# Sixteen leading blocks, plain block writes with accumulating gathers, and the shared expert's first products moved into TensorE's waits, in a recurrence-plus-MoE layer on one Trainium2 core

## Chip, cores and metric

The program runs on one NeuronCore of one Trainium2 chip. The metric is device time in microseconds. The kernel before takes 448.93 us, the median of three runs (447.82, 448.93, 449.15).

## What is computed

Input x is 4 sequences of 512 tokens with 256 features, all fp32. The layer is

```python
x = x + attn(layernorm(x))        # a gated complex linear recurrence over the 512 tokens
x = x + ffn(layernorm(x))         # a mixture of 32 experts and a shared expert
# ffn, for xf of 2048 tokens x 256:
scores = sigmoid(xf @ gate_w.T)                     # 32 experts in 8 groups
# the 4 groups with the highest maximum, in them the 6 best experts, weights normalised to 2.5
y = sum over the 6 chosen e of  w[e] * (silu(xf @ w11[e].T) * (xf @ w33[e].T)) @ w22[e].T
shared = (silu(xf @ sw1.T) * (xf @ sw3.T)) @ sw2.T  # inner width 256
out = y + shared
```

## The kernel before

Each engine has its own program, written out by hand: `block.sync` (SP, which only issues transfers), `gpsimd` (POOL), `scalar` (ACT), `vector` (DVE) and `tensor` (PE). Semaphores tie them together, so the order of the stages in each list is the order of the work.

**The front part** goes over the tokens in six chunks (`CHUNKS`, L45) of 256, 256, 512, 512, 256 and 256 tokens. For each chunk it makes the first layer norm, the projection, the gates, the recurrence (two scans on DVE), the output product (`residual_in`, L1106, and `out_project`, L1115), the second layer norm, the router's logits (`logits`, L1091) and scores, the choice of six experts (`choose`, L817) and, by products with a triangle of ones on PE (`positions`, L1125), the place of each token in its expert's list in DRAM (`places`, L859). Then POOL scatters the token's row to its six places (`scatter_rows`, L421): one indirect transfer for each tile of 128 tokens and choice, 96 in all, each of 128 rows of 320 floats (256 features, 32 weights and 32 row numbers).

**The table.** When all places are known, DVE works out which 128-row blocks of which expert are to be run in which order (L926 to L953), 127 blocks at most. The order runs by phases (`PHASE_ENDS`, L47), so that blocks holding early tokens come first. Three small products turn the table into a row (L1191 to L1193), which is copied to `tabs` (L955).

**The shared expert** is done by sequence b and half h: `shared_gate_up(b, h)` (L1160, four products of 512 columns), ACT's silu (L607), DVE's `shared_hidden` (L957), `shared_down(b)` (L1169, eight products of 256 columns) and DVE's `shared_out` (L962). In PE's program the pairs (0,0) and (0,1) stand behind the last `logits`, then `positions(4)` and `positions(5)`, the table, and all the rest.

**The loop over 127 blocks** is pipelined in steps. SP loads a block's rows (`load_block`, L352, up to eight ahead), PE transposes them (`rows_t`, L1216), multiplies by gate and up weights (`gate_up`, L1223) and by the down weights (`down`, L1232). ACT copies weights and takes silu. DVE multiplies (`hidden`, L982) and scales the output (`block_out`, L987). POOL scatters the 128 output rows to `choice_rows` in DRAM (`scatter`, L436), six rows a token side by side, one indirect transfer a block. When a phase is through, SP loads a tile's six rows a token (`load_choices`, L361, 768 KB), and DVE adds them to `resid` with six additions of 128x256 (`add_choice`, L1010), interleaved with the steps by `LOAD_AT` and `ADD_AT`. Tile 14 is summed on PE (L1261). Finished tiles are stored by ACT and SP.

Before its first block, SP waits for the table and for all 96 row scatters:

```python
            sp.wait_ge(s_tab, 1)
            sp.wait_ge(s_pad, 16)
            sp.wait_ge(s_outp, NCH)
            for i in range(NCH):
                sp.wait_ge(s_scat[i], 16 * TOPK * CHUNKS[i][2])
```

and PE waits for the four additions of the shared expert (`s_resid`) before the first transpose.

## Time and profile before

| | |
|---|---|
| three runs, median | 448.93 us |
| profiled execution: its own time | 450.83 us |
| profiled execution: span, first to last instruction | 449.1 us |
| PE busy / granted clock, mean | 376.1 us (84%) / 0.89 |
| DVE, ACT, POOL busy | 294.3, 260.7, 231.6 us |
| 127 scatters of block outputs on POOL | 127.0 us |
| 96 scatters of rows on POOL | 101.9 us |
| gate and up products of the blocks on PE | 134.9 us |

Times are from the span's start. A granted clock of 1.00 is 2.4 GHz, 0.50 is 1.2 GHz. In a timeline row the first number is the start, the second the length (of a merged run of instructions, start to end). In square brackets stands how long the engine had been idle before it and who released it.

### The profile page before, as it was taken

What the parts mean: (1) busy time and instruction counts of PE and PEld (TensorE: products, weight loads), DVE (VectorE), ACT (ScalarE), POOL (GpSimd) and SP (SyncE); (2) the same over time, 40 slices, a digit from 0 to 9 for tenths busy, and PEclk for the clock granted to TensorE, in tenths of its full rate; (3) what the DMA queues carried; (4) which work ended last, traced back from release to release, by engine and by line L of the source; (5) the groups of instructions that cost most, each with busy time, mean ns of one, the idle gap of its engine ahead of it and who ended that gap; (6) DMA issues with size and microseconds to landing.
All of it is one profiled execution on the core that took longest, in us unless ns stands there. A gap on an engine that the chain in (4) does not pass through costs nothing.

```text
span 449.1 us, 9145 instructions
## 1 busy us (share of the span) xinstructions
PE 376.1 (84%) x2120; PEld 301.2 (67%) x2121; DVE 294.3 (66%) x990; ACT 260.7 (58%) x585; POOL 231.6 (52%) x242
## 2 busy tenths in 40 slices
PE   2777696965976778399889999999999998998935
PEld 2644263745645563155579999999999997997924
DVE  3669688999988824612235555555567777777982
ACT  2678978768575132011157777767777776776710
POOL 2000000752778777777516666666656665663750
PEclk9898867595785687689999999999999999999996
DMA  8990000220335999333347666666689889879724
GB/s 241 405 339 2 0 0 1 74 102 15 118 118 201 413 430 380 130 128 128 117 145 215 188 195 182 204 188 191 191 265 354 255 248 300 303 208 336 244 83 174
DMA packets 41850, 87.70 MB, mean 195 GB/s; under 512 B 7204, under 2 KB 32295, under 8 KB 41296
## 3 DMA queue, kind: packets, MB, share of 16 engines
q1 hardware_dynamic: 28384, 54.77, 36.7%
q0 software_dynamic: 10704, 30.07, 18.6%
q10 hardware_dynamic: 2720, 2.40, 1.7%
q8 instruction: 15, 0.25, 0.3%
q14 instruction: 27, 0.22, 0.2%
HBM read 49.81 MB, written 39.71 MB: 199 GB/s over the span
## 4 chain that ended last, share of the span: by engine, by line
PE 50%; DVE 19%; ACT 9%; DMA 8%; issue 8%; POOL 3%; DVEq 1%; SPq 1%; ACTq 0%; POOLq 0%
PE PS L1228 17%; PE PS L1235 8%; PE PS L1165 7%; DMA payload_and_xn_t<-choice_rows 5%; PE PS L1220 4%; PE PS L1121 3%; POOL choice_rows L441 3%; PE PS L1178 3%; DMA resid<-in_x 2%; PE PS L1076 2%; ACT L605 1%; DVE st L682 1%; PE PS L1261 1%; ACT payload_and_xn_t L555 1%; DMA choice_rows<-block_out_s,block_meta 1%
## 5 line engine op out<-in xcount | busy, mean ns | idle before, releaser
L441 POOL DMA_INDIRECT choice_rows<-block_out_s,block_meta x127 | 127.0, 1000 | 86.0 <-issue 58.3
L427 POOL DMA_INDIRECT bucket_rows<-payload_and_xn_t,dest x96 | 101.9, 1062 | 116.2 <-DVE dest L874 88.2
L1228 PE MATMUL PS<-block_rows_t,block_gate_up_weights 128*128 128x128 f32 x1016 | 134.9, 276 | 0.0
L1228 PEld LDWEIGHTS PS<-block_rows_t,block_gate_up_weights 128*128 128x128 f32 x1016 | 123.4, 192 | 1.1 <-ACT block_rows_t L630 0.9
L625 ACT ACTIVATE block_gate_up_weights<-expert_weights 128x512 f32 x127 | 80.0, 630 | 35.6 <-issue 29.6
L1235 PE MATMUL PS<-expert_weights,block_hidden_t 128*128 x254 | 76.3, 382 | 3.8 <-DVE block_hidden_t L985 3.8
L992 DVE TENSOR_SCALAR block_out_s<-PS,block_meta 128x256 f32<-128x256 f32 x127 | 61.2, 482 | 0.0
L985 DVE TENSOR_TENSOR block_hidden_t<-block_silu_t,PS 128x128 f32<-128x128 f32 x127 | 36.3, 286 | 24.2 <-ACT block_silu_t L617 22.0
L630 ACT ACTIVATE block_rows_t<-PS 128x256 f32<-128x256 f32 x127 | 46.5, 366 | 7.6 <-PE PS L1220 7.6
L1220 PE MATMUL PS<-ident,block_rows_s 128*128 128x128 f32 x254 | 48.6, 273 | 1.4 <-DVE resid L964 1.3
L980 DVE COPY block_meta<-block_rows_s 128x2 f32 x127 | 22.0, 173 | 41.7 <-issue 41.4
L617 ACT ACTIVATE block_silu_t<-PS 128x128 f32<-128x128 f32 x127 | 35.0, 276 | 18.7 <-PE PS L1228 18.0
L1220 PEld LDWEIGHTS PS<-ident,block_rows_s 128*128 128x128 f32 x254 | 35.6, 141 | 14.5 <-DVE resid L964 1.7
L1016 DVE TENSOR_TENSOR resid<-resid,payload_and_xn_t 128x256 f32<-128x256 f32 x90 | 37.8, 421 | 10.1 <-DMA payload_and_xn_t<-choice_rows 9.2
L1235 PEld LDWEIGHTS PS<-expert_weights,block_hidden_t 128*128 128x128 f32 x254 | 38.5, 192 | 4.9 <-issue 4.9
L1165 PE MATMUL PS<-payload_and_xn_t,sw_s 128*128 128x512 f32 x64 | 33.3, 676 | 1.2 <-DVE turn_abs L960 1.2
L1121 PE MATMUL PS<-w_in_and_w_out,block_rows_s 128*128 128x256 f32 x96 | 25.8, 418 | 0.4 <-DVE block_rows_s L797 0.4
L1165 PEld LDWEIGHTS PS<-payload_and_xn_t,sw_s 128*128 128x128 f32 x64 | 13.8, 219 | 17.8 <-issue 16.0
L1076 PE MATMUL PS<-expert_weights,gate_blockdiag 128*128 128x256 f32 (+1 forms) x48 | 22.6, 634 | 1.7 <-ACT expert_weights L499 1.5
L1121 PEld LDWEIGHTS PS<-w_in_and_w_out,block_rows_s 128*128 128x128 f32 x96 | 20.3, 213 | 4.6 <-issue 0.7
L605 ACT ACT_TABLE_LOAD x18 | 23.1, 1283 | 0.3
L1087 PE MATMUL PS<-ident,payload_and_xn_t 128*128 128x128 f32 x32 | 7.4, 392 | 15.9 <-ACT payload_and_xn_t L555 12.0
(185 smaller groups left out, 459.1 us busy)
## 6 DMA issues: line engine op xcount, KB each, us to landing
block_rows_s<-bucket_rows SPq DMA_DIRECT2D x127, 160.0 KB
payload_and_xn_t<-choice_rows SPq DMA_DIRECT2D x16, 768.0 KB, 6.5
bucket_rows<-pad_rows SPq DMA_DIRECT2D x1, 5120.0 KB, 26.3
expert_weights<-in_experts SPq DMA_DIRECT2D x1, 4224.0 KB, 14.0
expert_weights<-in_experts SPq DMA_DIRECT2D x1, 3456.0 KB, 16.3
expert_weights<-in_experts SPq DMA_DIRECT2D x1, 2688.0 KB, 18.3
resid<-in_x SPq DMA_DIRECT2D x4, 512.0 KB, 9.3
choice_rows<-block_out_s,block_meta POOLq DMA_INDIRECT x127, 3.2
```

Source lines behind the costliest of these rows:

```text
L427: nc.gpsimd.indirect_dma_start(out=bucket_ap[:, :], out_offset=bass.IndirectOffsetOnAxis(ap=dest[:, t, k:k + 1], axis=0), in_=PAY[:, t, :] ...
L441: nc.gpsimd.indirect_dma_start(out=choice_ap[0:rows, :], out_offset=bass.IndirectOffsetOnAxis(ap=meta_id[:, slot, 1:2], axis=0), in_=yy[:, ...
L625: A(ws[:, r, :], W[:, bass.ds(first, KD * 2 * P)], ACT.Copy)
L630: A(xT[:, r, :], PS[:, r, 0:D], ACT.Copy).then_inc(s_xt, 1)
L985: TT(hh[:, r, :], sg[:, r, :], PS[:, 2 + r, P:2 * P], M).then_inc(s_hh, 1)
L992: TSC(yy[:, slot, :], PS[:, 6 + r, 0:D], meta[:, weight, 0:1], None, M).then_inc(s_y, 1)
L1016: ins = TT(resid[:, n, :], resid[:, n, :], RINGS[:, n % RING, k, :], AD)
L1121: ins = mm(PS[:, 6 + t // 2, (t % 2) * D:(t % 2 + 1) * D], PROD[h][:, t * P:(t + 1) * P], wt, start=False, stop=(n == len(parts) - 1 and t ...
L1165: ins = mm(PS[:, bank, :], sw13_s[:, k, g, h * P:(h + 1) * P], XN2T[:, b, k, :], start=(k == 0), stop=(k == KD - 1))
L1220: ins = nc.tensor.transpose(PS[:, r, k * P:(k + 1) * P], xs[:, slot, k * P:(k + 1) * P], ident[:])
L1228: ins = mm(PS[:, 2 + r, g * P:(g + 1) * P], ws[:, r, (2 * k + g) * P:(2 * k + g + 1) * P], xT[:, r, k * P:(k + 1) * P], start=(k == 0), st ...
L1235: mm(PS[:, 6 + r, 0:D], hh[:, r, :], W[:, bass.ds(w + KD * 2 * P, D)], start=True, stop=True).then_inc(s_yp, 1)
```

## The change

1. **Row format.** A row is 288 floats, with no row numbers. `choose` loses the scan and the addition that made them. It is cut in two stages, `choose_groups` and `choose_experts`.
2. **Block outputs.** SP writes each block's output with a plain transfer to 128 consecutive rows of `bucket_outputs`, at a row from a fourth row of the table (`write_block`, 11 blocks behind its load). SP reads its table entries four at a time. POOL's 127 scatters go. The tensor is cleared first, by five transfers from a zero tile.
3. **Token sums.** POOL gathers a tile's output rows, one indirect transfer for each choice, 96 of 128x256 in all. Choices 0 and 3 are added by the transfer into `resid`, 4 and 5 into the copies that 1 and 2 have made. DVE then makes two additions a tile in place of six. PE's sum and ACT's stores go, and SP stores. The places of the rows are worked out on DVE (`output_rows`, `output_sources`). Tile n is gathered once its phase is written and tile n - 4 is added.
4. **Leading blocks.** The first 16 blocks are full blocks of the first 8 tiles, found by `early_blocks`. SP loads them once the rows of chunks 0 to 2 have landed, and waits for the others before block 16. There are nine phases in place of five.
5. **Shared expert.** On PE the gate product of (0,0) goes before `residual_in(5)`, its up product between `ln2_transpose(4)` and `logits(4)`, and the two passes of (0,1)'s gate product into the gaps around `ln2_transpose(5)`. DVE makes the hidden rows of (0,0) and (0,1) between the stages of the last router chunks. The table's product stands behind the fifth pair.
6. **Loops** run over 8 steps in place of 16, and further.

```diff
-    PHASE_ENDS = (1, 2, 3, 4, 5)
+    CUTS = [[2], [2], [2, 4], [2, 4], [2], [1, 2]]
+    PHASE_TILES = [b * TS + t0 + cut for (b, t0, nt), cuts in zip(CHUNKS, CUTS) for cut in cuts]
...
+    RING = 4
+    SUMS = 3
+    EARLY_BLOCKS = 16
+    EARLY_TILES = 8
+    FIRST_ADD = 67
+    WRITE_LAG = NXS + 3
...
         def blocks_through(phase):
+            return max((PHASE_TILES[phase] * P * TOPK + E * (P - 1)) // P, EARLY_BLOCKS + E)
...
+            for n in range(NCH - 1):
+                part = slice(n * BLOCKS // (NCH - 1), (n + 1) * BLOCKS // (NCH - 1))
+                sp.wait_ge(s_gp, n + 1)
+                sp.dma_start(outputs_ap[part.start * P:part.stop * P].rearrange("(j p) d -> p j d", p=P),
+                             PADT[:, 0:D].unsqueeze(1).to_broadcast([P, part.stop - part.start, D])).then_inc(s_clear, 16)
...
+            rows_scattered(0, early_chunks)
...
+            def write_block(j, u):
+                if u % 4 == 0:
+                    sp.reg_load(first_outputs, tabs[0:1, bass.ds(j + 3 * P, 4)])
+                sp.wait_ge(s_y, j + 1)
+                row = sp.snap(first_outputs[u % 4], min_val=0, max_val=2 * P * P - P)
+                sp.dma_start(outputs_ap[bass.ds(row, P), :], yy[:, u % NY, :]).then_inc(s_ys[u % NY], 16)
...
+            for j in range(EARLY_BLOCKS):
+                load_block(j, j, j - NXS + 1 if j >= NXS else None)
+                if j >= WRITE_LAG:
+                    write_block(j - WRITE_LAG, j - WRITE_LAG)
+            rows_scattered(early_chunks, NCH)
...
+            def gather_outputs(n):
+                all_written(pool, blocks_through(phase_of(n)))
+                pool.wait_ge(s_src, n // TS + 1)
...
+                if n >= RING:
+                    pool.wait_ge(s_added, added(n - RING))
+                for k in range(TOPK):
+                    part = k % SUMS
+                    landed = s_cin[n % RING][part]
+                    into = resid[:, n, :] if part == 0 else RINGS[:, n % RING, part - 1, :]
+                    if k >= SUMS:
+                        pool.wait_ge(landed, 16 * (TOPK // SUMS) * (n // RING) + 16)
+                    nc.gpsimd.indirect_dma_start(
+                        out=into, out_offset=None, in_=outputs_ap[0:BLOCKS * P, :],
+                        in_offset=bass.IndirectOffsetOnAxis(ap=source[:, n, k:k + 1], axis=0),
+                        compute_op=ALU.add if part == 0 or k >= SUMS else ALU.bypass).then_inc(landed, 16)
...
-                dve.wait_ge(s_memb, i + 1)
-                flat_memb = memb[:, CHUNKS[i][1]:CHUNKS[i][1] + nt, :].rearrange("p t e -> p (t e)")
-                c.add(V.tensor_tensor_scan(rank[:, n, :].rearrange("p t e -> p (t e)"), flat_memb, flat_memb, 0.0, AD, ALU.bypass))
-                c.wait()
-                c.add(STT(PAY_id[:, rows, D + 1::2], rank[:, n, :], float((NT - 1 - tile) * P * TOPK),
...
-                    (ln2_stats, 5), (ln2_shift, 5), (choose, 4), (choose, 5), (places, 4), (places, 5)):
+                    (ln2_stats, 5), (ln2_shift, 5), (choose, 4), (choose_groups, 5),
+                    (first_product, 0), (choose_experts, 5), (places, 4), (first_product, 1), (places, 5),
+                    (early_blocks, 0)):
...
-            c.add(TT(PICKS, quant[:], PER_V.unsqueeze(1).to_broadcast([P, 3, V5]), M))
+            shared_out(0)
+            shared_hidden(1, 1)
+            c.add(TT(PICKS, quant[:], PER_V.unsqueeze(1).to_broadcast([P, 4, V5]), M))
...
+            def add_at(u, turn=None):
+                tile, k = u // (2 * TOPK) * 2 + u % (2 * TOPK) // ADDS, u % ADDS
+                if u % (2 * TOPK) < 2 * ADDS:
+                    add_sum(tile, k, turn)
...
-                    (out_project, 4), (positions, 3), (residual_in, 5), (out_project, 5), (ln2_transpose, 4),
-                    (logits, 4), (ln2_transpose, 5), (logits, 5)):
+                    (out_project, 4), (positions, 3), (first_gate, 0), (residual_in, 5), (out_project, 5),
+                    (ln2_transpose, 4), (first_up, 0), (logits, 4), (second_gate, 0), (ln2_transpose, 5),
+                    (second_gate, 1), (logits, 5)):
...
+            shared_part(0, 1, 1)
             positions(4)
+            shared_gate_up(1, 0)
             positions(5)
...
             for b in range(B):
-                if b + 1 < B:
+                if 0 < b and b + 1 < B:
                     shared_gate_up(b + 1, 0)
                 shared_down(b)
                 if b + 1 < B:
                     shared_gate_up(b + 1, 1)
+                if b == 1:
+                    block_table()
```

PE's program before, from the last `positions` ahead of the gap (L1135) to the products of the shared expert (L1165). `sw_s` are the shared expert's weights, `payload_and_xn_t` the normalised tokens:

```order
L1135 MATMUL PS<-member,ones 128x32 x4
L1111 MATMUL PS<-bout_s,ones_row 128x512
L1113 MATMUL PS<-resid,ident 128x256 x2
L1121 MATMUL PS<-w_in_and_w_out,block_rows_s 128x256 x4
L1121 MATMUL PS<-w_out_n,block_rows_s 128x256 x2
L1121 MATMUL PS<-w_in_and_w_out,block_rows_s 128x256 x2
L1087 MATMUL PS<-ident,payload_and_xn_t 128x128 x4
L1099 MATMUL PS<-gwt_s,payload_and_xn_t 128x32 x4
L1087 MATMUL PS<-ident,payload_and_xn_t 128x128 x4
L1099 MATMUL PS<-gwt_s,payload_and_xn_t 128x32 x4
L1165 MATMUL PS<-payload_and_xn_t,sw_s 128x512 x8
```

and the same place in the changed program (its lines L1289 are the shared expert's products):

```order
L1289 MATMUL PS<-payload_and_xn_t,sw_s 128x512 x2
L1257 MATMUL PS<-bout_s,ones_row 128x512
L1259 MATMUL PS<-resid,ident 128x256 x2
L1267 MATMUL PS<-w_in_and_w_out,block_rows_s 128x256 x4
L1267 MATMUL PS<-w_out_n,block_rows_s 128x256 x2
L1267 MATMUL PS<-w_in_and_w_out,block_rows_s 128x256 x2
L1233 MATMUL PS<-ident,payload_and_xn_t 128x128 x4
L1289 MATMUL PS<-payload_and_xn_t,sw_s 128x512 x2
L1245 MATMUL PS<-gwt_s,payload_and_xn_t 128x32 x4
L1289 MATMUL PS<-payload_and_xn_t,sw_s 128x512
L1233 MATMUL PS<-ident,payload_and_xn_t 128x128 x4
L1289 MATMUL PS<-payload_and_xn_t,sw_s 128x512
```

Six of the eight products that stood behind the last logits now stand in four places before them, two, two, one and one.

SP's program before, at the first two blocks. Each block reads the table once (L358) and issues one transfer:

```order
L358 TENSOR_LOAD tabs
L358 ISA x2
L359 ISA
L359 DMA block_rows_s<-bucket_rows 128x320
L358 TENSOR_LOAD tabs
```

and in the changed program, from the part of the loop that also stores tiles (`bucket_outputs` is what `write_block` writes, `out` the result):

```order
L382 TENSOR_LOAD tabs
L386 ISA
L387 DMA block_rows_s<-bucket_rows 128x288
L394 ISA
L395 DMA bucket_outputs<-block_out_s 128x256
L404 DMA out<-resid 128x256
L386 ISA
L387 DMA block_rows_s<-bucket_rows 128x288
L394 ISA
L395 DMA bucket_outputs<-block_out_s 128x256
```

SP now issues two transfers a block, or three where a tile is stored, and reads the table twice for four blocks, once for the loads and once for the writes.

## Rows read from the trace of the kernel before

**Rows 1.** Stretches of the loop on PE: length, PE busy, granted clock, DMA share, GB/s.
```profile
240.00:280.00 40.00, 40.00 (x313) 1.00 0.65 197
360.00:400.00 40.00, 38.49 (x293) 1.00 0.85 269
```

**Rows 2.** Timeline of PE, steps of the loop: start, length, line, operation, tiles.
```profile
230.31 0.38 PE L1220 MATMUL PS<-ident,block_rows_s 128*128 128x128 f32 x2
231.86 0.38 PE L1220 MATMUL PS<-ident,block_rows_s 128*128 128x128 f32 x2
...
426.83 0.38 PE L1220 MATMUL PS<-ident,block_rows_s 128*128 128x128 f32 x2
```

**Rows 3.** Waits in the loop: who waited for whom, us in total, times, longest.
```profile
PE PS L1235 <- DVE block_hidden_t L985: 3.8, 4, 1.5
```

**Rows 4.** Timeline of PE between the last positions and the loop.
```profile
153.03 2.04 PE L1111 MATMUL PS<-bout_s,ones_row 1*128 1x512 f32 x2 [2.03 <-ACT resid L546]
...
156.88 3.08 PE L1121 MATMUL PS<-w_in_and_w_out,block_rows_s 128*128 128x256 f32 x8
...
163.87 1.08 PE L1099 MATMUL PS<-gwt_s,payload_and_xn_t 128*128 128x32 f32 x8 [1.75 <-ACT payload_and_xn_t L562]
...
168.55 9.28 PE L1165 MATMUL PS<-payload_and_xn_t,sw_s 128*128 128x512 f32 x16
...
185.45 0.58 PE L1191 MATMUL PS<-ident,tabf 128*1 128x128 f32 x2 [6.02 <-DVE tabf L953]
...
188.12 6.31 PE L1165 MATMUL PS<-payload_and_xn_t,sw_s 128*128 128x512 f32 x8 [1.23 <-DVE turn_abs L960]
...
208.04 7.03 PE L1165 MATMUL PS<-payload_and_xn_t,sw_s 128*128 128x512 f32 x16
...
228.40 0.95 PE L1220 MATMUL PS<-ident,block_rows_s 128*128 128x128 f32 x4 [1.31 <-DVE resid L964]
```

**Rows 5.** Timeline of the end: PE's last down product, last output on DVE, last store.
```profile
430.74 0.69 PE L1235 MATMUL PS<-expert_weights,block_hidden_t 128*128 x2 [0.79 <-DVE block_hidden_t L985]
431.70 0.48 DVE L992 TENSOR_SCALAR block_out_s<-PS,block_meta 128x256 f32<-128x256 f32 x1
446.93 0.34 ACTq L668 DMA_DIRECT2D out<-block_rows_s  x1
```

**Rows 6.** Timeline of SP's queue, the first two loads.
```profile
224.26 1.48 SPq L359 DMA_DIRECT2D block_rows_s<-bucket_rows  x2
```

**Rows 7.** The indirect transfers on POOL: duration ns min/median/max, first and last start; then block outputs' landing.
```profile
L427 POOL DMA_INDIRECT bucket_rows<-payload_and_xn_t,dest x96: 956/960/2452, 79.4 to 220.7; - x96
L441 POOL DMA_INDIRECT choice_rows<-block_out_s,block_meta x127: 983/983/1242, 233.5 to 433.8; - x127
DMA to landing us min/median/max: 2.3/3.2/7.0
```

**Rows 8.** Two stretches on PE before and after its idle time at 151.
```profile
150.00:152.00 2.00, 0.77 (x16) 1.00 0.79 332
154.00:156.00 2.00, 2.00 (x4) 0.50 0.99 417
```

**Rows 9.** Timeline of DVE: row numbers, second norm, last places, the table's widest product.
```profile
150.55 0.41 DVE L855 TENSOR_TENSOR_SCAN rank<-member 128x128 f32<-128x128 bf16 x1
...
151.21 0.76 DVE L682 BATCH_NORM_STATS2 st<-PS 128x6 f32<-128x256 f32 x2
...
161.72 0.76 DVE L682 BATCH_NORM_STATS2 st<-PS 128x6 f32<-128x256 f32 x2 [5.55 <-PE PS L1121]
...
180.31 0.17 DVE L874 TENSOR_SCALAR dest<-dest_sorted 128x12 int32<-128x12 f32 x1
...
183.58 0.66 DVE L946 TENSOR_TENSOR block_rows_s<-block_quantities,block_rows_s 128x480 f32<-128x480 f32 x1
```

**Rows 10.** Timeline of ACT behind the last scores.
```profile
170.08 1.28 ACT L632 ACT_TABLE_LOAD   x1
```

**Rows 11.** The page, busy share of the DMA engines in tenths, 40 slices of 11.2 us.
```profile
DMA  8990000220335999333347666666689889879724
```

522 lines of the change are left out of this document (308 added, 214 removed).

## The prediction

> **What bounds the kernel now.** I read the stretches first, then the waits, then PE's timeline. The program has three parts. In the loop PE is the bound: it is busy all 40 us of a stretch [rows 1], and a step takes 231.86 - 230.31 = 1.55 us [rows 2] (1.546 by rows that repeat). From the third block's transpose to the last one's are 124 steps in 426.83 - 230.31 = 196.5 us [rows 2], where 124 x 1.546 would be 191.7, so the loop gives away 4.8 us, 3.8 of it where DVE, held up by its additions of loaded choices, brings `hidden` late [rows 3]. The first transpose starts at S = 228.4 and the last down product ends at T = 430.74 + 0.69 = 431.4 [rows 4, 5], so T - S = 203.0. The tail from T to the end at 449.1 is 17.7 us. Before S a chain of PE, ACT and DVE sets the time, and two things end together there: PE's first transpose waits for DVE's last shared addition [rows 4], and SP's loads start at 224.26 [rows 6], when the last of POOL's 96 scatters (start 220.7, 0.96 long [rows 7]) has landed. So neither the shared expert nor the scatters can be shortened alone. The change takes both.
>
> **Last out product.** PE idles 2.03 us at 151.0 and its granted clock falls from 1.00 to 0.50 [rows 4, 8]. `residual_in(5)` and half of `out_project(5)` then run at 1.2 GHz: bias and residual take 156.88 - 153.03 = 3.85 us, where the same instructions take 1.7 at full clock (two of 512 columns at 7.03 / 16 = 0.43, four of 256 at half of that, 0.22 [rows 4]). `first_gate` is four instructions of 512 columns, 1.7 us, and fits into the gap, so I expect the clock to stay at 2.4 GHz. The row numbers that `choose` loses cost DVE 151.21 - 150.55 = 0.66 us for a chunk of four tiles [rows 9], so what PE waits for comes 0.65 earlier. Then the residual ends at 152.75 + 1.7 = 154.5, DVE's products are there, and the out product takes 16 x 0.22 = 3.5: it ends at 158.0 in place of 161.7 [rows 9]. Gain 3.7.
>
> **Router of the last chunk.** `first_up` (1.7 us) fits into the wait of 1.75 before `logits(4)` [rows 4]. The two single passes (0.86 each) lie at ACT's norm and copy and may push `logits(5)` by 0.5. In DVE's order `first_product(0)` now stands ahead of `choose_experts(5)`. It waits for ACT's table load (1.28 [rows 10]) and silu, some 1.2 us, and everything of chunk 5 queues behind it. But before, `positions(4)` stood behind 9.28 us of products [rows 4], and now behind 1.7. By this schedule the last place is known at 174.1 in place of 180.5 [rows 9], so 2.7 more than the 3.7.
>
> **From the last place to the loop.** Before: 228.4 - 180.5 = 47.9 us, with PE idle 6.02 for the table and 1.23 behind it, and a pair at half clock, 6.31 in place of 7.03 / 2 = 3.5 [rows 4]. Now DVE has `early_blocks` (22 operations, mostly of 128 columns: the old table, 21 operations of 160 columns, took from 180.5 to 185.4 [rows 4, 9], so I take 4.7 us), then a table of 288 columns (6.3), then a product and a reduction of 1,152 columns (by 0.66 for 480 [rows 9], 1.35 each), and small ones. PE meanwhile does `shared_down(0)`, (1,1) and (2,0), and waits some 4.7 us for the hidden rows of (1,1), which stand in the middle of DVE's table work. After that PE has (2,1), the table, (3,0), down 2, (3,1), down 3 at 3.5 each, and DVE's `output_rows` (five operations of 512 columns, 4.1 us with the small ones) fits beside them. I get S = 212.0. The wait of 4.7 is long enough for the clock to fall, as the one of 6.02 did, and I add one pair at half clock, 3. The row numbers of chunks 0 to 2 come off a DVE that is over 90% busy there, 1.8 us in all, and I take 1.5 off. **S = 213.5, a gain of 14.9.** Loads must not stop this: SP's wait is now for chunk 2's scatters, which end near 161. The others may end at 224 as before: block 16 is wanted at 213.5 + 1.9 + 15 x 1.55 = 238.6, over 10 us later. Clearing 16.6 MB and the smaller rows cost nothing as long as the DMA engines are idle, as they are in the four slices from 34 to 79 us [rows 11]. Lost, that cover would only delay POOL, which has those 10 us.
>
> **The loop.** DVE has 32 additions in place of 90 and more, each placed 15 and more steps after its phase, so the 4.8 us go down to some 0.8: **T - S = 199.0, a gain of 4.0.** SP issues two transfers a step. A load came every 1.14 us (1.48 less one issue of 0.34 [rows 6]), of which 0.8 was the reading of the table. With two readings for four blocks that makes (8 x 0.34 + 2 x 0.8) / 4 = 1.1 us, with waits 1.2, under 1.55. If reading four entries saved nothing it would be 2 x 1.14 = 2.3, and the loop SP's, which the listed instructions speak against.
>
> **Gathers.** No row shows an accumulating gather. The nearest is the scatter of an output block: 0.98 on POOL plus the 0.30 that always lie between two, landing in 3.2, at most 7.0 [rows 7]. Below, a gather may cost the 0.96 of a row scatter. Above, the added reading of the destination may double the landing to 6.4. I take the scatter's values: choice 3 waits for choice 0's landing (3.2), which three issues (3 x 1.28 = 3.8) cover, so a tile takes t = 7.7. The pairs of tiles come every 12 steps (18.6 us), so POOL (15.4) keeps up. The engines' share was 0.65 without and 0.85 with the 768 KB loads [rows 1]. The same 12.6 MB now come in 1 KB rows, over more steps. The Trainium skill ("DMA: Bandwidth & Descriptors", Bandwidth) says to batch transfers to 1 MiB for over 75% of peak, which speaks against replacing 768 KB loads by 128 KB gathers. By that rule the gathers would land late under a filled set of engines, and the sum would be that of rival (a). The rows of before neither confirm nor deny it.
>
> **The tail.** Block 114 is written 13.6 us before T (its output at T + 0.75 - 12 x 1.55, and SP issues the write only after the load of block 125, plus landing). From there POOL gathers tiles 12 and 13 until T + 2, then tile 14 (which waits for tile 10's additions, the last of the loop) until T + 9.7, and tile 15's last gather starts at T + 16.1. Landing 3.2, one addition 0.4, store 449.1 - 446.93 = 2.2 [rows 5]: **T + 22.0, a loss of 4.3** against 17.7.
>
> **Sum.** 449.1 - 14.9 - 4.0 + 4.3 = 434.5 for the span. The median of the runs, 448.93, is 0.2 below this span (the profiled execution's own time, 450.83, is 1.9 above the median), so the time is **434.3 us**.
>
> **Rivals.**
> (a) *Gathers set the end, slower.* If an accumulating gather lands in L over 3.9 us, choices 3, 4 and 5 each wait for it and a tile takes L + 3.9. POOL starts at S + 81.8 (block 47 written), and the end is S + 81.8 + 16 (L + 3.9) - 1.3 + L + 2.75 = S + 145.7 + 17 L. It decides from L = 4.4, is slower than before from L = 5.4, and at L = 6 gives 461. For it: landings up to 7.0 under load [rows 7], two reads for each write. Against it: the median of 3.2 at nearly the same rate. The same page (SWDGE vs HWDGE vs iDMA) says that DVE in its two-port mode locks GpSimd out of the memory in which it writes descriptors. Here POOL's instruction rose to 2.45 once in the front part, but not above 1.24 in the loop [rows 7], and DVE does less there now. Chance 0.17, with a loop held by SP or the DMA engines (each 0.1 us a step is 13 us) in it.
> (b) *The front part gives little.* If `first_gate` runs long or late, the clock falls all the same, and DVE's longer table work (some 14 us more than before with the output rows) sets S: the 3.7 and half of the 10 go, S = 222, end 443. Chance 0.15.
> (c) *No effect.* The leading blocks do nothing unless the table comes before the scatters' end, and the gain of the front would be eaten by a tail of 30 us: 448 to 450. Chance 0.04.
> (d) *More gain.* No second fall of the clock (-3), gathers landing in 2.3 and issued in 0.96 (-2), no wait left in the loop (-1): 428 or less. Chance 0.08.
> The forecast, 428 to 440, has 0.56.
>
> **Numbers.** A measurement of this kernel tells about 0.3% from no change. Faster than that: forecast, (b) and (d), 0.79. Slower: 0.17. Within: 0.04. The range of 8 in 10 runs from 427, which leaves out part of (d), to 451, which takes in (a) up to L = 5.4 and leaves out the rest.
>
> **What would show it.** Right: the last out product's end near 158, with the clock at 1.00 over `residual_in(5)`. The first transpose near 213, released by the shared addition. Steps of 1.546 with no wait for `hidden`. The first load before the last row scatter. POOL's gathers 1.28 apart and its last one starting some 16 us after T. Wrong: a first transpose after 220, POOL waiting on a landing in front of choice 3, a step longer than 1.6, or an end over 25 us behind T.

## The result, and the profile after

| | before | after |
|---|---|---|
| median of four runs each | 448.94 us | 477.44 us |
| profiled execution: own time / span | 450.83 / 449.1 us | 478.19 / 476.4 us |
| first transpose of the loop, S | 228.4 | 214.9 |
| loop, T - S | 203.0 | 425.6 - 214.9 = 210.7 |
| tail behind T | 17.7 | 50.8 |

The change makes the kernel slower: ratio 1.0634, 95% interval 1.0597 to 1.0671. I had forecast 434.3 us and a range up to 451.

PE's timeline after the change, in the places of [rows 4] and [rows 2] (start, length of the merged run, in square brackets the idle time before it and its releaser):

```profile
151.60 1.96 PE L1289 MATMUL PS<-payload_and_xn_t,sw_s 128*128 128x512 f32 x4
153.49 1.12 PE L1257 MATMUL PS<-bout_s,ones_row 1*128 1x512 f32 x2
154.54 1.13 PE L1259 MATMUL PS<-resid,ident 128*128 128x256 f32 x4
...
158.10 1.03 PE L1267 MATMUL PS<-w_in_and_w_out,block_rows_s 128*128 128x256 f32 x4
...
189.82 3.72 PE L1345 MATMUL PS<-sw_s,w_in_and_w_out 128*128 128x256 f32 x16 [3.50 <-DVE w_in_and_w_out L948]
...
214.90 0.44 PE L1388 MATMUL PS<-ident,block_rows_s 128*128 128x128 f32 x2 [1.32 <-DVE resid L952]
...
424.89 0.69 PE L1403 MATMUL PS<-expert_weights,block_hidden_t 128*128 x2 [0.34 <-DVE block_hidden_t L1122]
```

The gap of 2.03 us in front of the last residual is filled, and the product of 1x512 that took 2.04 us now takes 1.12. The out product ends at 159.1 (161.7 before), and the first transpose starts 13.5 us earlier. The front part did most of what was forecast (14.9 us).

Groups of instructions by line on POOL (busy us, mean ns of one; then the idle time before them), which answer to [rows 7]:

```profile
L489 POOL DMA_INDIRECT payload_and_xn_t<-bucket_outputs,output_rows x64 | 80.9, 1264 | 19.5 <-issue 16.2 <-DMA bucket_outputs<-block_out_s 2.4 <-DMA payload_and_xn_t<-bucket_outputs,output_rows 0.6
L489 POOL DMA_INDIRECT resid<-bucket_outputs,output_rows x32 | 49.8, 1556 | 98.2 <-issue 83.7 <-DMA resid<-bucket_outputs,output_rows 14.5
```

The 32 gathers into `resid` all add, and take 1.556 us of POOL each. Those into the ring, 1.264 in the mean, are half plain and half adding. One tile in POOL's timeline shows the two kinds apart:

```profile
341.94 1.53 POOL L489 DMA_INDIRECT resid<-bucket_outputs,output_rows  x1 [0.30 <-issue]
343.77 1.00 POOL L489 DMA_INDIRECT payload_and_xn_t<-bucket_outputs,output_rows  x1 [0.30 <-issue]
345.08 0.97 POOL L489 DMA_INDIRECT payload_and_xn_t<-bucket_outputs,output_rows  x1 [0.30 <-issue]
347.69 1.57 POOL L489 DMA_INDIRECT resid<-bucket_outputs,output_rows  x1 [1.64 <-DMA resid<-bucket_outputs,output_rows]
349.57 1.55 POOL L489 DMA_INDIRECT payload_and_xn_t<-bucket_outputs,output_rows  x1 [0.30 <-issue]
351.42 1.53 POOL L489 DMA_INDIRECT payload_and_xn_t<-bucket_outputs,output_rows  x1 [0.30 <-issue]
353.26 1.53 POOL L489 DMA_INDIRECT resid<-bucket_outputs,output_rows  x1 [0.30 <-issue]
...
467.92 1.53 POOL L489 DMA_INDIRECT payload_and_xn_t<-bucket_outputs,output_rows  x1 [0.30 <-issue]
```

Choices 1 and 2, plain, cost 0.97 to 1.00 us; choices 0, 3, 4 and 5, which add, 1.53 to 1.57. Choice 3 also waits until choice 0 has landed; here it starts 5.75 us after choice 0. This tile takes 11.3 us where I had put 7.7. In the tail, with the loop over, choice 3 no longer waits:

```profile
429.77 1.53 POOL L489 DMA_INDIRECT resid<-bucket_outputs,output_rows  x1 [0.30 <-issue]
...
434.18 1.58 POOL L489 DMA_INDIRECT resid<-bucket_outputs,output_rows  x1 [0.30 <-issue]
```

There a tile takes 10.0 us, all of it issuing. The first gather starts at 298.36 and the last at 467.92, and in these 169.6 us POOL is never idle for longer than 2.0 us: the chain of gathers runs without a break almost to the end.

The same stretches as [rows 1] (columns: bounds and length; PE, PEld, DVE, ACT, POOL busy with their counts; granted clock, DMA share, GB/s):

```profile
240.00:280.00 40.00, 40.00 (x312) 37.41 (x311) 22.43 (x78) 30.12 (x79) 0.00 (x0) 1.00 0.61 181
...
320.00:360.00 40.00, 38.68 (x291) 35.25 (x291) 22.80 (x81) 27.70 (x73) 28.84 (x22) 1.00 1.01 261
360.00:400.00 40.00, 35.18 (x250) 31.53 (x248) 20.36 (x70) 23.65 (x63) 30.10 (x23) 0.96 0.96 224
```

Until the gathers run the loop is at PE's full pace. From 320 on it loses time, and DVE's timeline shows how:

```profile
385.09 0.15 DVE L1117 COPY block_meta<-block_rows_s 128x1 f32 x1 [0.60 <-issue]
388.84 0.42 DVE L1161 TENSOR_TENSOR resid<-resid,payload_and_xn_t 128x256 f32 x1 [3.59 <-DMA payload_and_xn_t<-bucket_outputs,output_rows]
389.18 0.28 DVE L1122 TENSOR_TENSOR block_hidden_t<-block_silu_t,PS 128x128 f32<-128x128 f32 x1
```

An addition stands at a fixed step, the gather that it waits for is late, and the hidden rows (L1122) queue behind it. PE waits 3.16 us for them at 389.6, and 6.2 us in the whole loop.

My theory from here on is **A**: an adding gather costs POOL 1.56 us instead of 0.97, and this, with the wait for choice 0's landing, makes the chain that sets the end; the loop's loss is a consequence beside the path. The rivals: **B**, the landing sets the pace whatever the gather's kind; **C**, the DMA engines are full and hold everything; **D**, the loop's loss is itself the cause.

### The profile page after: what moved, and what is told of

It is laid out like the page before. It is cut to its first block, busy times and chain, and to the rows that moved or that the text cites. A ratio compares the mean times of both kernels' runs of the same rounds, so it can differ in the third digit from the quotient of the medians.

```text
span 476.4 us, 9521 instructions
## 1 busy us (share of the span) xinstructions
PE 367.2 (77%) x2113; PEld 294.7 (62%) x2114; DVE 286.0 (60%) x986; ACT 262.0 (55%) x584; POOL 233.7 (49%) x209
## 4 chain that ended last, share of the span: by engine, by line
PE 52%; DVE 11%; ACT 10%; DMA 8%; POOL 8%; issue 7%; DVEq 1%; SPq 1%; ACTq 1%; POOLq 1%
PE PS L1396 18%; PE PS L1403 9%; PE PS L1388 4%; POOL payload_and_xn_t L489 4%; PE PS L1267 4%; PE PS L1289 4%; POOL resid L489 3%; DMA payload_and_xn_t<-bucket_outputs,output_rows 3%; DMA resid<-bucket_outputs,output_rows 2%; PE PS L1345 2%; PE PS L1245 2%; PE PS L1259 2%; PE PS L1257 2%; DMA resid<-in_x 2%; DVE st L709 2%
## 5 line engine op out<-in xcount | busy, mean ns | idle before, releaser
L468 POOL DMA_INDIRECT bucket_rows<-payload_and_xn_t,dest x96 | 100.5, 1047 | 117.2 <-DVE dest L906 88.9
L489 POOL DMA_INDIRECT resid<-bucket_outputs,output_rows x32 | 49.8, 1556 | 98.2 <-issue 83.7
L489 POOL DMA_INDIRECT payload_and_xn_t<-bucket_outputs,output_rows x64 | 80.9, 1264 | 19.5 <-issue 16.2
L1403 PE MATMUL PS<-expert_weights,block_hidden_t 128*128 x254 | 78.0, 389 | 6.6 <-DVE block_hidden_t L1122 6.2
L1117 DVE COPY block_meta<-block_rows_s 128x1 f32 x127 | 19.6, 154 | 57.6 <-issue 57.0
L1122 DVE TENSOR_TENSOR block_hidden_t<-block_silu_t,PS 128x128 f32<-128x128 f32 x127 | 36.4, 287 | 26.6 <-ACT block_silu_t L659 24.0
L1403 PEld LDWEIGHTS PS<-expert_weights,block_hidden_t 128*128 128x128 f32 x254 | 38.8, 193 | 9.2 <-issue 8.5
L1161 DVE TENSOR_TENSOR resid<-resid,payload_and_xn_t 128x256 f32 (+1 forms) x32 | 13.6, 425 | 50.4 <-DMA payload_and_xn_t<-bucket_outputs,output_rows 48.7
L1289 PE MATMUL PS<-payload_and_xn_t,sw_s 128*128 128x512 f32 x64 | 31.3, 629 | 2.9 <-DVE turn_abs L948 2.9
L1267 PE MATMUL PS<-w_in_and_w_out,block_rows_s 128*128 128x256 f32 x96 | 24.8, 404 | 0.0
L1222 PE MATMUL PS<-expert_weights,gate_blockdiag 128*128 128x256 f32 (+1 forms) x48 | 21.2, 599 | 2.2 <-ACT expert_weights L541 1.5
L1289 PEld LDWEIGHTS PS<-payload_and_xn_t,sw_s 128*128 128x128 f32 x64 | 12.2, 199 | 15.0 <-issue 11.6
```

Source lines behind the costliest of these rows:

```text
L468: nc.gpsimd.indirect_dma_start(out=bucket_ap[:, :], out_offset=bass.IndirectOffsetOnAxis(ap=dest[:, t, k:k + 1], axis=0), in_=PAY[:, t, :] ...
L489: nc.gpsimd.indirect_dma_start(out=into, out_offset=None, in_=outputs_ap[0:BLOCKS * P, :], in_offset=bass.IndirectOffsetOnAxis(ap=source[: ...
L1122: TT(hh[:, r, :], sg[:, r, :], PS[:, 2 + r, P:2 * P], M).then_inc(s_hh, 1)
L1267: ins = mm(PS[:, 6 + t // 2, (t % 2) * D:(t % 2 + 1) * D], PROD[h][:, t * P:(t + 1) * P], wt, start=False, stop=(n == len(parts) - 1 and t ...
L1289: ins = mm(PS[:, bank, :], sw13_s[:, k, g, h * P:(h + 1) * P], XN2T[:, b, k, :], start=(k == 0), stop=(k == KD - 1))
L1403: mm(PS[:, 6 + r, 0:D], hh[:, r, :], W[:, bass.ds(w + KD * 2 * P, D)], start=True, stop=True).then_inc(s_yp, 1)
```

## The experiments: what sets the end

All runs of this section stood beside runs of the kernel before that took 448.7 to 449.2 us. Three kernels, the changed one and the next two, tell the theories apart by the kind of the gathers alone.

**All gathers plain.** Order, waits and additions of DVE are those of the changed kernel.

```diff
-                        compute_op=ALU.add if part == 0 or k >= SUMS else ALU.bypass).then_inc(landed, 16)
+                        compute_op=ALU.bypass).then_inc(landed, 16)
```

> The changed kernel with all its gathers plain, in the same order, with the same waits and the same additions of DVE (so the sums lack choices 0, 3, 4 and 5's adding), beside a kernel before that takes 449. Theory A (an adding gather costs POOL 1.55 us, a plain one 0.97): a tile costs 7.6 us of POOL, POOL idles between phases, T - S falls to about 199, the last gather starts some 16 us after T and the time is 437 (433 to 442). Rival C (the DMA engines' contention holds the gathers, whatever their kind): over 465.

**Two of six adding.** The same line with `compute_op=ALU.add if part == 0 else ALU.bypass`.

> The changed kernel with two adding and four plain gathers a tile (the sums lack choices 1 and 2), beside a kernel before that takes 449. Theory A: 8.9 us a tile against 10.0 with four adding ones (10.7 with its waits), so POOL's chain is 142 us if it never idles; the phases come every 18.6 us for two tiles, so POOL idles a little and the end is 20 to 27 us below the changed kernel's 477: 450 to 457. By a fixed cost for each gather whatever its kind it would be 477.

Measured: all plain 445.93 us (ratio to before 0.9936, interval 0.9912 to 0.996), half 460.81 (1.0266, 1.023 to 1.0302), beside the 477.44 of the changed kernel. The groups on POOL, first all plain, then half:

```profile
L489 POOL DMA_INDIRECT payload_and_xn_t<-bucket_outputs,output_rows x64 | 60.7, 948 | 25.1 <-issue 13.1 <-DMA payload_and_xn_t<-bucket_outputs,output_rows 6.9 <-DMA bucket_outputs<-block_out_s 4.8
L489 POOL DMA_INDIRECT resid<-bucket_outputs,output_rows x32 | 30.5, 953 | 97.4 <-DMA bucket_outputs<-block_out_s 76.5 <-DMA resid<-bucket_outputs,output_rows 15.9 <-issue 4.7
```

```profile
L489 POOL DMA_INDIRECT payload_and_xn_t<-bucket_outputs,output_rows x64 | 62.3, 974 | 21.3 <-issue 15.8 <-DMA bucket_outputs<-block_out_s 3.6 <-DMA payload_and_xn_t<-bucket_outputs,output_rows 1.9
L489 POOL DMA_INDIRECT resid<-bucket_outputs,output_rows x32 | 50.5, 1577 | 96.5 <-issue 81.3 <-DMA resid<-bucket_outputs,output_rows 14.6 <-DMA bucket_outputs<-block_out_s 0.6
```

The instruction falls from 1.56 us to 0.95 when it stops adding, and only then. Making 32 adding gathers plain gives 16.6 us, the other 32 another 14.9: 31.5 us together. POOL's busy time in the chain falls by more, 38.8 us, but POOL is then held up 5.7 us longer (17.7 us instead of 12.0, beside the 0.3 between two gathers), and the end lies 1.6 us further behind the last gather's start. T - S is 199.7 with all plain (414.47 - 214.82).

Both kernels lie 4 us above the upper end of what I had expected, since POOL does not idle between phases. With all plain, from the first gather (298.45) to the last (434.96) are 136.5 us, where 95 times 1.25 is 119. The waits for choices 0 to 2 to have landed make up 15 of the difference (15.9 + 6.9 in the two rows, in 26 of them, each holding the 0.3 that always lies between two). So B had a part in the pace. It explains little of what lies between 445.93 and the forecast of 434.3, though, since the forecast had the chain at 133.3 us, with POOL idle between phases. By the spans (445.0 against 434.5) 1.3 us lie in front of S, 1.8 between S and the first gather, 3.2 in the chain and 4.1 behind the last gather's start. The version with five places, further down, has no landing wait on POOL, and its chain takes 136.4 us too.

C falls as well. With all plain the DMA share was 0.92 from 320 to 360 and 0.94 from 360 to 400, and PE was busy 39.8 and 40.0 of the 40 us. And in the tail of the changed kernel, with a DMA share of 0.51 to 0.55, an adding gather still took POOL 1.53 to 1.58 us.

**Additions later.** `FIRST_ADD` 67 to 75 and `FIRST_STORE` 80 to 88, nothing else.

> The changed kernel with every addition of DVE in the loop, and the store behind it, 8 steps (12.4 us) later. Nothing is left out. Theory A (POOL's chain of gathers sets the end by itself, and the loop's own loss of some 12 us comes from additions that stand in DVE's order ahead of the hidden rows and wait for gathers which run behind their schedule): T - S falls from 211 to about 200, the waits of PE for the hidden rows go, POOL's first gather to its last still takes 170 us, and the time stays within 3 us of the changed kernel's. Rival D (the loop's loss delays the block outputs that the gathers need and is itself the cause): the time falls by as much as T - S does, some 10 us, with the gathers' chain shorter than 165 us.

Measured 477.72 us (1.0611, 1.0554 to 1.0668), as long as the changed kernel. PE's last product and POOL's first and last gather:

```profile
416.71 0.69 PE L1403 MATMUL PS<-expert_weights,block_hidden_t 128*128 x2 [0.67 <-DVE block_hidden_t L1122]
```

```profile
298.28 1.60 POOL L489 DMA_INDIRECT resid<-bucket_outputs,output_rows  x1 [76.26 <-issue]
...
468.12 1.53 POOL L489 DMA_INDIRECT payload_and_xn_t<-bucket_outputs,output_rows  x1 [0.30 <-issue]
```

T - S falls from 210.7 to 202.6, the chain still takes 169.8 us, and the time does not move. D falls: 8 us less in the loop change nothing at the end.

**No leading blocks.** SP's first load waits for all 96 scatters: `rows_scattered(0, early_chunks)` becomes `rows_scattered(0, NCH)`.

> The changed kernel, but SP's first load waits for all 96 row scatters, as before the change. Nothing is left out. Theory A: the scatters end as late as before the change, so the first load comes some 22 us later than with leading blocks (there 199.65 in the trace of the changed kernel, last scatter near 221), S and all behind it move by 8 to 12 us, the first gather follows S by 83.5 us as ever, and the time is 8 to 12 us longer. If rival (c)'s premise holds (the leading blocks do nothing), S and the time stay within 2 us.

Measured 489.37 us (1.0881, 1.082 to 1.0943), 11.9 above the changed kernel.

```profile
222.46 1.23 PE L1387 MATMUL PS<-ident,block_rows_s 128*128 128x128 f32 x4 [10.57 <-DMA block_rows_s<-bucket_rows]
```

PE waits 10.57 us for its first block, and S is 7.6 us later. The first gather follows at 308.44, 10.1 later than in the changed kernel and so not at the fixed distance from S that I had expected. The chain itself takes 170.6 us. So the leading blocks are worth 11.9 us, and a later start of the gathers moves the end.

**First gate product moved back**, behind `ln2_transpose(4)`:

```diff
-                    (out_project, 4), (positions, 3), (first_gate, 0), (residual_in, 5), (out_project, 5),
-                    (ln2_transpose, 4), (first_up, 0), (logits, 4), (second_gate, 0), (ln2_transpose, 5),
+                    (out_project, 4), (positions, 3), (residual_in, 5), (out_project, 5),
+                    (ln2_transpose, 4), (first_gate, 0), (first_up, 0), (logits, 4), (second_gate, 0), (ln2_transpose, 5),
```

> The changed kernel with its first gate product moved from in front of the last residual to behind the last-but-one transposes of ln2, with nothing left out; beside a kernel before that takes 449. By my prediction's step the clock then falls to 0.50 over the residual and half of the out product, the out product ends 3 us later, S moves from 214.9 to 218 and, since the gathers follow S by 83.5 us, the time from 477.4 to 480 or 481. If DVE's table work sets S by then (rival (b)'s premise), less than 1 us.

Measured 482.89 us (1.0757, 1.07 to 1.0814), 5.5 above the changed kernel, where I had expected 3 to 4; by the spans 4.1. The last out product's first eight matmuls and the stretch around them:

```profile
156.07 3.57 PE L1267 MATMUL PS<-w_in_and_w_out,block_rows_s 128*128 128x256 f32 x8
...
219.05 0.44 PE L1388 MATMUL PS<-ident,block_rows_s 128*128 128x128 f32 x2 [1.31 <-DVE resid L952]
```

```profile
154.00:156.00 2.00, 2.00 (x6) 0.78 (x5) 1.97 (x7) 1.25 (x3) 1.63 (x2) 0.97 0.68 288
156.00:158.00 2.00, 1.93 (x5) 1.57 (x6) 1.04 (x4) 0.00 (x0) 1.45 (x2) 0.50 1.14 485
```

With the gap open again the clock falls to 0.50, later than in the kernel before (156 instead of 152), and eight matmuls take 3.57 us where they took 1.89. The first transpose is 4.15 later, the first gather 4.1.

But the 4.15 are not the price of this gap alone. The last logits end 3.65 later (169.19 against 165.54): 1.7 by the eight slow matmuls, and about as much because the gate product now stands in their way. From there on the clock falls at other places than in the changed kernel, here first the changed kernel's rows and then those of this run:

```profile
170.36 5.40 PE L1289 MATMUL PS<-payload_and_xn_t,sw_s 128*128 128x512 f32 x8 [2.91 <-DVE turn_abs L948]
...
189.82 3.72 PE L1345 MATMUL PS<-sw_s,w_in_and_w_out 128*128 128x256 f32 x16 [3.50 <-DVE w_in_and_w_out L948]
```

```profile
173.49 3.70 PE L1289 MATMUL PS<-payload_and_xn_t,sw_s 128*128 128x512 f32 x8 [2.38 <-DVE turn_abs L948]
...
191.21 6.48 PE L1345 MATMUL PS<-sw_s,w_in_and_w_out 128*128 128x256 f32 x16 [3.46 <-DVE w_in_and_w_out L948]
```

In the changed kernel the pair in front of the last positions runs partly at half clock and the product behind the wait of 3.50 us at full clock. Here it is the other way round. So the last place is known only 1.4 us later, and 2.8 of the 4.15 arise at the second product. In the other eight undisturbed kernels of this family the second product was slow in four (5.41 us), and the wait in front of it was 3.5 to 3.6 us in all eight. The filled gap keeps the clock up over the out product, then. What that is worth at the end, no run here separates.

## The experiments: a version that keeps the gain

**Six plain gathers into six planes.** The full sum, with DVE adding six times a tile and no landing wait on POOL:

```diff
-    ADDS = SUMS - 1
+    ADDS = TOPK
...
-                    into = resid[:, n, :] if part == 0 else RINGS[:, n % RING, part - 1, :]
-                    if k >= SUMS:
-                        pool.wait_ge(landed, 16 * (TOPK // SUMS) * (n // RING) + 16)
+                    into = RINGS[:, n % RING, k, :]
...
-                        compute_op=ALU.add if part == 0 or k >= SUMS else ALU.bypass).then_inc(landed, 16)
+                        compute_op=ALU.bypass).then_inc(landed, 16)
```

> The changed kernel with six plain gathers a tile into six planes of the ring and six additions of DVE a tile, two behind each pair of landings, so that the output is the full sum; beside a kernel before that takes 449. Theory A: gathers at 7.6 us a tile, T - S about 201 because DVE has 96 additions again, a tail of 24 us, so 439 (435 to 444), below both kernels. Rival B (the landing sets the pace): 450 and more.

Measured 459.3 us (1.0218, 1.0179 to 1.0257): a miss by 20. POOL's part held, 0.964 us a gather and 7.55 a tile, but it now waits for others: 21.1 us for block outputs, 13.3 for DVE. SP's queue shows one cause (line L404 is the store of a tile):

```profile
331.14 0.34 SPq L395 DMA_DIRECT2D bucket_outputs<-block_out_s  x1
338.04 0.34 SPq L404 DMA_DIRECT2D out<-resid  x1
338.65 0.35 SPq L387 DMA_DIRECT2D block_rows_s<-bucket_rows  x1
```

SP stands 6.6 us at the store of tile 1, whose additions now end 11 steps behind the first of tile 0 and no longer 3, and no load or write goes out meanwhile. PE waits 4.7 us for block rows. I had left the stores' places as they were. The next three runs mend this and two other places, each on top of the one before.

**Stores at step 88 in place of 80:**

> The version with six plain gathers a tile, with SP's stores of finished tiles moved from step 80 to step 88 and nothing else. If its missing 20 us come from SP, which at its 80th load waits for additions of tile 1 that end only at DVE's step 78 and so keeps the next block rows and output writes back (PE waited 4.7 us for block rows, POOL 21 us for block outputs), T - S falls from 210.4 to about 202 and the time from 459 to 447 (443 to 451). If DVE's 96 additions, waiting for gathers ahead of the hidden rows, are the cause, it stays at 457 to 460.

452.61 us (1.0056, 1.0017 to 1.0095), 6.7 less, where I had expected 12. T - S is 205.5, and POOL's wait for block outputs 12.0.

**A ring of five places** (`RING = 5`, the two loops with additions and stores written out):

> As the one with the later stores, with five places in the ring in place of four and the additions and stores written out instead of looped. POOL's waits for DVE (13.3 us in the version with four places) should go, tile 14 no longer waits for tile 10's additions but for tile 9's at T, and the last gather starts at T + 17 instead of T + 22: 3 to 6 us below the one with the later stores, about 442, which would be below the kernel before's 449. If code loading of the longer written-out part costs, it is slower than that one.

445.91 us (0.9923, 0.9887 to 0.9959), 6.7 less again, where I had expected 442. T - S is 198.7, and POOL's wait for DVE 5.5.

**One more phase**, `CUTS` for chunk 4 `[1, 2]` in place of `[2]`:

> As the one with five places, and the phase of tiles 12 and 13 cut in two, so that tile 12's gathers may start some 6 steps (9 us) earlier. POOL had been idle in front of that phase if its tiles take 7.6 us and the phases come every 18.6, so the tail shrinks by up to 7 us: 434 to 440. The table before the loop has 320 columns in place of 288, which costs DVE some 0.5 us in front of S. If POOL's chain is full there anyway, no gain.

442.7 us (0.9855, 0.9805 to 0.9906), a miss too, with 434 to 440 expected. Its tail is 28.7 us (T = 415.5), with POOL's tiles 13 to 15 end to end:

```profile
412.01 0.94 POOL L480 DMA_INDIRECT payload_and_xn_t<-bucket_outputs,output_rows  x1 [0.30 <-DMA bucket_outputs<-block_out_s]
...
434.10 0.95 POOL L480 DMA_INDIRECT payload_and_xn_t<-bucket_outputs,output_rows  x1 [0.30 <-issue]
```

It is 6.5 us (1.5%) faster than the kernel before and 35 faster than the changed one. Its interval overlaps with that of the version with five places, so the last step's own gain is not shown. S is 216.4 in the profiled execution, in place of 213.9 with five places, and 1.7 us of this are the granted clock and not the wider table:

```profile
189.68 5.41 PE L1331 MATMUL PS<-sw_s,w_in_and_w_out 128*128 128x256 f32 x16 [3.49 <-DVE w_in_and_w_out L939]
```

The same 16 products took 3.72 us with five places. The profiled execution, 445.92 us, is also the longest of the six. Of what it lacks of the forecast (a span of 444.2 against 434.5) 2.9 us lie in front of S, 0.1 in the loop and 6.7 in the tail.

## The experiments in a disturbed time

The first runs of the study fell in a time in which the kernel before took 535 to 536 us instead of 449, on three chips; one of these gave 449 again six minutes later. They stand apart from the others, since they do not measure the same thing.

> The changed kernel, with all six gathers of a tile plain in place of four of them adding. Same number of transfers, bytes, waits and additions on DVE; it leaves out the adding of choices 0, 3, 4 and 5, so these are not summed. Theory A (POOL's own time for an adding gather, 1.55 us in place of 0.97, fills POOL: 10.0 us a tile and 11.1 with waits, 16 tiles end to end from 298 to 470): a tile takes 6 x 1.28 = 7.7 us, POOL idles between pairs of tiles, the end is 22 us behind PE's last down product, span about 437. Theory B (the transfers themselves are slow: 1 KB rows fill the DMA engines whether they add or not): landings stay at 4 to 5 us, a tile stays at 9.5 or more with waits, span over 460.

> The changed kernel with the whole sum kept but no adding gather: six plain gathers of a tile into six planes of the ring, and DVE makes six additions a tile, one in each step from step 67. Theory A: as the run with plain gathers, 7.7 us a tile. Tile 10's last four additions fall behind the loop, 1.7 us, so the tail is some 2 us longer: span 439 to 441, faster than the kernel before by 2%. Theory B: over 460. A third theory (DVE's additions are the cost that the change rightly took away): steps near 1.6 us and waits of PE for hidden rows of over 5 us, span 445 to 450.

> The same kernel with six plain gathers a tile once more, since in the first call all engines paused together for 1 to 3 us many times, in the kernel before too (536 us in place of 449), so that its times say little. Theory A (POOL's time for an adding gather): 7.7 us a tile, POOL idle between pairs, tail some 24 us, span 439 to 441 against 449 of before. Theory B (transfers slow whether they add or not): over 460. Third theory (DVE's additions): 445 to 450 with waits of PE for hidden rows of over 5 us.

> The kernel before, with only this part of the change: the first gate product before residual_in(5), the first up product before logits(4). The clock should stay at 1.00 over residual_in(5) and the last out product end near 158.7 in place of 161.7. Theory A (the front is bound twice, by PE's chain and by POOL's 96 scatters): the first load cannot come before 224.3, the first transpose comes at 226.5 to 227 in place of 228.4, gain 1.5 to 2 us, 447. Rival (the scatters have slack): the first transpose comes 3 us or more earlier, at 225.4 or before, 446 or less. Second rival: no gain at all, since the time between the last place and the loop grows by as much.

> The changed kernel with the first gate product moved back from before residual_in(5) to behind ln2_transpose(4). If the product's worth lies in the granted clock of residual_in(5) and out_project(5): clock 0.50 there again, last out product ends 3 us later (162 in place of 159.0), first transpose at 218 in place of 214.9, and, as POOL's gathers start at a fixed distance behind it, end 3 us later, 480.5. Rival: the order alone mattered, and the last out product ends at most 1 us later.

> The changed kernel unaltered, as the yardstick for runs in which the kernel before takes about 536 us. Theory A (POOL's own time for an adding gather sets the end): 32 + 32 adding gathers at 1.55 us, tiles 10 to 11 us apart, POOL without idle from the first gather to the last. If the kernel before takes 449 again, this one takes 477; if it takes 536, I expect about 530, since the kernel with its first gate product moved back took 528 there, and the ratio to before says only how the pauses fall on the two kernels.

> The changed kernel with only choices 0 and 3 gathered by adding, choices 4 and 5 by plain gathers over choices 1 and 2 (so the sums lack choices 1 and 2). Theory A (an adding gather costs POOL 1.55 us, a plain one 0.97): a tile costs 2 x 1.86 + 4 x 1.28 = 8.8 us with the waits it keeps up to 10, so 0.6 x 32 = 19 us and more come off POOL's chain and the end is 15 to 22 us before that of the changed kernel. Rival B (the landing of the gathers sets the end, their kind does not matter): the same time as the changed kernel within 3 us. Rival C (contention of the DMA engines): in between, with POOL idle in front of tiles.

| disturbed time | us | ratio to before, interval | T - S | the same undisturbed |
|---|---|---|---|---|
| all plain | 588.55 | 1.0986, 1.0902 to 1.1069 | 301.2 | 199.7 |
| six planes | 580.41 | 1.0855, 1.0788 to 1.0922 | 287.6 | 210.4 |
| six planes, other chip | 566.99 | 1.0623, 1.0565 to 1.068 | 284 | 210.4 |
| before with first gate and up moved | 538.15 | 1.0054, 1.0016 to 1.0093 | 259.2 | (before: 203.0) |
| first gate moved back | 528.01 | 0.974, 0.9666 to 0.9813 | 215.3 | 211.1 |
| half adding | 524.73 | 0.9761, 0.9664 to 0.9859 | 240.3 | 200.8 |
| changed kernel | 513.99 | 0.9591, 0.9489 to 0.9693 | 211.8 | 210.7 |

Even the sign turns: here the changed kernel is 4% faster than the one before. ACT's timeline in the half adding one shows what happens (`remote` is a releaser that the profile does not know):

```profile
366.55 0.37 ACT L672 ACTIVATE block_rows_t<-PS 128x256 f32<-128x256 f32 x1
369.25 0.28 ACT L659 ACTIVATE block_silu_t<-PS 128x128 f32<-128x128 f32 x1 [2.33 <-PE PS L1396]
369.74 0.63 ACT L667 ACTIVATE block_gate_up_weights<-expert_weights 128x512 f32 x1 [0.21 <-issue]
370.71 0.38 ACT L672 ACTIVATE block_rows_t<-PS 128x256 f32<-128x256 f32 x1 [0.34 <-remote]
```

PE, ACT and DVE stop together for about 2 us (before 370, ACT is idle for 2.33 us, DVE for 2.59 and PE for 1.86) while POOL issues indirect transfers, and POOL itself goes on at 1.28 us. Between 345 and 481, 17 of the 63 steps that ACT's rows show are longer than 2.5 us. From 280 to 320, before the first gather, PE is busy all 40 us. The growth of the loop goes with the kind of transfers beside it, though these runs were on different chips: T - S grows by 74 to 101 us with 96 plain gathers, by 40 with 64 of them, by 56 with the 127 plain scatters of the old loop, and by 1 to 4 with 32 plain among 64 adding gathers. Why, the runs don't show. What they do confirm of theory A: POOL's instruction took 1.56 us adding and 0.96 plain here too, and the changed kernel's chain took 170.0 us (334.08 to 504.05), as undisturbed, while the loop beside it could hardly have been more different. The front-only and gate-back runs decide nothing: in the first, PE stood still for 11.6 us at the very place that their edit is about, and the front part alone was not run again undisturbed. So what the front part gives by itself in the kernel before is not shown. The expectations in microseconds of these seven runs were all missed for this reason, and what counts are the undisturbed runs above of five of these six kernels.

## Why the prediction was wrong

The span came out 41.9 us above the sum: 1.4 in front of S, 11.7 in the loop, 28.8 behind T. Step by step:

- **Last out product.** Forecast end 158.0 with the clock at 1.00; 159.1 with the clock at 1.00. Right, with 1 us missing, since `first_gate` took until 153.5.
- **Router of the last chunk.** Last place forecast for 174.1, known at 177.0 (DVE's wait of 2.51 for the last positions). The gain was 3.5 and not 6.4. In front of the last positions stands a pair of shared products that waited 2.91 us for DVE and then took 5.40 us, with the clock at 0.50 from 172 to 174, where it took 3.70 in the run with the gate product moved back.
- **From the last place to the loop.** Forecast 39.4 us, 38.0 measured; the wait for the hidden rows of (1,1) was 3.50 against 4.7. I had put a fall of the clock behind this wait, and in the profiled execution it came in front of the last positions instead. S = 214.9 against 213.5. The run with the gate product moved back confirms that the filled gap keeps the clock over the out product; how much of its 5.5 us is due to that stays open.
- **Leading blocks.** The first load went out at 199.65, before the last scatter, and SP kept ahead of PE. Taking the lead away cost 11.9.
- **The loop.** Forecast T - S 199.0. All plain it is 199.7, so the loop was sized rightly, and SP's loads came every 1.13 us (223.78, 224.91, 226.04), with a write between them. With adding gathers it is 210.7, by additions that wait for late gathers. The later additions took 8 of these 12 away and the time stayed: this miss is off the path.
- **Gathers: the step that failed.** "I take the scatter's values": 0.98 on POOL and a landing of 3.2, t = 7.7. I had bounded POOL's time from below by 0.96 and put all that adding could cost above it on the landing, up to twice; I never asked what it costs POOL to issue. Measured: 4 x (1.86 - 1.28) = 2.3 us for the adding, and 0.7 for waits, because choice 3 could start only 5.2 to 6.1 us after choice 0 in nine of the ten tiles where it waited (landing at a median of 5.0 us and not 3.2, and 4.2 with all plain). 7.7 + 2.3 + 0.7 = 10.7 us a tile, and 10.0 of it without any wait. The DMA share from 360 to 400 was 0.96 where [rows 1] had 0.85, although the bytes read for the sums were the same. The Trainium skill ("DMA: Bandwidth & Descriptors", Bandwidth) says to batch transfers to 1 MiB, which I had set aside. By that rule gathers of 128 KB fill the engines more than loads of 768 KB do, and the trace of the all plain kernel agrees: a share of 0.94 at 275 GB/s from 360 to 400, against 0.85 at 269 before. From 240 to 280, without either, they were alike (0.61 at 181 and 0.65 at 197).
- **Tail.** Forecast T + 22.0 with POOL's pairs of tiles at 15.4 in a phase of 18.6. At 10.7 a tile they are 21.4, over the phase, so POOL falls behind from the first pair on and never idles. Chain start S + 83.5 (forecast 81.8), chain 169.6 (forecast to the last start 133.3), from there to the end 8.5 (5.9): 1.7 + 36.3 + 2.6, with the 1.4 of S the whole 42. Most of the last 2.6 is the last store, 4.2 us from its issue to the end where I had taken 2.2.

Rival (a), gathers end to end that set the end, is what came, at 0.17. Its place and its sum by 16 tiles end to end were right, and its trigger was not: I let it hang on the landing alone, with 5.4 us as the point where it gets slower. POOL's own 1.56 us brings the tile to 10.0 even if the landing is hidden. The lock of DVE against POOL, which I had named beside it, did not show: in the tail, where DVE was busy 0.9 of 10 us, an adding gather took 1.53 to 1.58 us, as it did in the loop (1.60 at most). In the front part of the kernel before ten of the 96 scatters took longer than 1.3 us and not only the one of 2.45; what held them up is not shown.

## What to carry to other kernels

Price a new kind of instruction on the engine that issues it as well as where it lands: an operation that "comes free with the transfer" may cost the issuing engine over half as much again (1.56 us in place of 0.97 here), and if that engine is to work in phases, compare its time for a phase with the phase's length first. Here the gathers had 15.4 of 18.6 us, and 1.2 times would have been enough to make POOL the bound. When a stage is given more work per item, every instruction placed for it at a fixed step on another engine (an addition, a store) has to be moved too, or it stops what is queued behind it. At SP this cost 6.7 us of the time, at DVE 8 us of the loop, which here lay off the path.

## What the hardware showed that I had not expected

- An indirect gather of 128x256 floats took POOL 0.95 to 1.00 us plain and 1.55 to 1.57 us with an addition, as medians of every run, disturbed or not (single ones up to 1.22 and 1.75).
- Choice 0's gather landed within 4.4 us of its start in the tail (no wait in front of choice 3 there, DMA share 0.55), and choice 3 had to wait in the loop until 5.2 to 6.1 us behind choice 0's start in nine of ten tiles, where the share was 1.01 from 320 to 360.
- Behind the same wait of PE of 3.5 us the granted clock fell to 0.50 in some profiled executions and stayed at 1.00 in others (5.41 us and 3.72 us for the same 16 products), in kernels whose edits are about other places. One profiled execution does not show which of the two a kernel gets.
- In the disturbed time plain indirect transfers on POOL went together with stops of PE, ACT and DVE of about 2 us, and the loop whose gathers were two thirds adding was hardly touched. The order of the kernels turned round. A comparison of two kernels holds only beside a run of the old one in the same minutes.
- From the end of the last store's issue to the end of the span were 1.8 us in the kernel before (447.3 to 449.1), 3.8 in the changed kernel (472.6 to 476.4) and 6.5 in the all plain one (438.5 to 445.0). Why stays open.
